# Twelve buffers of fetched edge rows, and sums stored nine steps behind the fetches

## What is computed

```python
h = relu(layernorm(x))
x = x + layer0(h, edge scalars 16, edge vectors 4, gather by src, sum by dst)
h = relu(layernorm(x))
x = x + layer1(h, edge vectors 3, edge features 64, gather by dst, sum by src)

# inside a layer, for every edge e
w   = act(edge_features[e] @ Wfc1) @ Wfc2        # 192 or 224 weights of the edge
f   = node_features[other end of e]              # 160 values of a node
msg = products of w, f and the edge's 3-vector   # 449 or 640 columns
agg[own end of e] += msg                         # segment sum over nodes
```

## Time and profile before

| | |
|---|---|
| time, median of 3 runs | 12249.92 us (12239.58 to 12279.39) |
| the profiled execution, its own time | 12298.2 us |
| its span, first to last instruction | 12296.4 us |
| messages of layer 0, first load to the end of the stage | 2794 to 7956 us |
| messages of layer 1 | 8718 to 12013 us |
| busy: PE, DVE, ACT, POOL | 60%, 61%, 41%, 59% of the span |
| the 16 DMA engines | 107 GB/s on the mean |

### The profile page before, as it was taken

The page is one execution under the profiler, slowest core; times in us unless marked ns, Lnnn a source line. Parts: engine busy times, 40 slices in busy tenths (PEclk is TensorE's granted clock), DMA queues, the critical chain, the costliest instruction groups (busy, mean ns, idle before and its releaser), DMA issues. The chain is left out here.

```text
span 12296.4 us, 187070 instructions
## 1 busy us (share of the span) xinstructions
PE 7410.2 (60%) x31320; PEld 4866.9 (40%) x31320; DVE 7443.2 (61%) x21099; ACT 4992.3 (41%) x16585; POOL 7196.8 (59%) x7101
## 2 busy tenths in 40 slices
PE   4444444445555555555555555577667777777777
PEld 3222222222222222222222222255566666666667
DVE  6444444445565565555555565576667777777763
ACT  2333333333333333333333333343445555555553
POOL 4666666656666666666666666555555666665650
PEclk7555555557777777777777777788899999999999
DMA  2222222223333333333333334444444444444465
GB/s 80 74 74 74 73 73 72 74 69 108 106 109 107 109 110 108 108 109 107 107 108 109 109 108 108 92 148 143 120 116 127 128 122 124 128 128 122 129 114 166
DMA packets 854401, 1321.82 MB, mean 107 GB/s; under 512 B 253376, under 2 KB 655040, under 8 KB 854208
## 3 DMA queue, kind: packets, MB, share of 16 engines
q0 software_dynamic: 339456, 670.10, 20.0%
q1 hardware_dynamic: 469232, 606.08, 17.5%
q10 hardware_dynamic: 45648, 44.94, 1.3%
HBM read 868.56 MB, written 918.54 MB: 145 GB/s over the span
## 5 line engine op out<-in xcount | busy, mean ns | idle before, releaser
L1396 POOL DMA_INDIRECT feat_m<-feat_tab,rows_m x3744 | 3867.9, 1033 | 2929.9 <-DMA rows_m<-sorted_rows 1401.3
L1470 PE MATMUL bank<-prod_m,hot_m 128*128 128x449 f32 x3744 | 2329.6, 761 | 2211.0 <-issue 646.9
L1493 PE MATMUL pair<-prod_m,hot_m 128*128 128x160 f32 x14976 | 2386.6, 316 | 930.1 <-DVE prod_m L1679 621.6
L1493 PEld LDWEIGHTS pair<-prod_m,hot_m 128*128 128x128 f32 x14976 | 2203.1, 201 | 1114.1 <-issue 1114.0
L1526 ACT ACTIVATE prod_m<-part_m,rows_m 128x64 f32<-128x64 f32 x5616 | 1442.4, 337 | 2812.9 <-DVE part_m L1665 1890.2
L1514 ACT ACTIVATE hot_m<-hot_m,rows_m 128x128 f32<-128x128 f32 x5616 | 1742.7, 388 | 1565.9 <-DVE hot_m L1648 1194.7
L600 POOL DMA_INDIRECT sorted_rows<-rows_e,place_e x1664 | 1634.9, 983 | 1051.8 <-issue 520.7
L1470 PEld LDWEIGHTS bank<-prod_m,hot_m 128*128 128x128 f32 x3744 | 858.1, 252 | 3446.1 <-issue 3285.3
L1413 POOL DMA_INDIRECT sorted_rows<-later_m,place_m x1248 | 1274.2, 1021 | 380.9 <-issue 369.9
L1711 DVE SCALAR_TENSOR_TENSOR acc_m<-acc_m,same_block,bank 128x449 f32<-128x449 f32 x936 | 636.5, 680 | 1294.6 <-remote 731.3
L1679 DVE TENSOR_TENSOR prod_m<-rows_m,feat_m 128x192 f32<-128x192 f32 (+1 forms) x4680 | 1226.9, 311 | 0.0
(11 more groups left out here) (241 smaller groups left out, 8767.3 us busy)
## 6 DMA issues: line engine op xcount, KB each, us to landing
agg_tab<-acc_m SPq DMA_DIRECT2D x936, 320.0 KB
rows_m<-sorted_rows SPq DMA_DIRECT2D x936, 229.0 KB
agg_tab<-acc_m SPq DMA_DIRECT2D x936, 224.5 KB
rows_m<-sorted_rows SPq DMA_DIRECT2D x936, 197.0 KB
feat_m<-feat_tab,rows_m POOLq DMA_INDIRECT x3744
turned_m<-in_turned ACTq DMA_DIRECT2D x159, 256.0 KB
agg_s<-agg_tab SPq DMA_DIRECT2D x98, 320.0 KB, 2.7
sorted_rows<-rows_e,place_e POOLq DMA_INDIRECT x1664
```

The lines of the kernel that those rows point to most:

```text
L1396: pool.indirect_dma_start(out=feat[s % RING][:, k, :], out_offset=None, in_=g.feat_tab[l.n], in_offset=bass.IndirectOffsetOnAxis(ap=rows[s ...
L1470: mm = pe.matmul(out[:, 0, :], hot[s % HOTS][:, k, 0, :], prod[s % prods][:, k, 0:l.agg], start=(k == 0), stop=(k == ST_TILES - 1))
L1493: mm = pe.matmul(dst, hot[s % HOTS][:, k, q, :], rhs, start=(k == 0 and col == 0), stop=(k == ST_TILES - 1), skip_group_check=True)
```

## The change

The rows get a ring of twelve buffers, the gathered features keep six under a name of their own (FRING), and the store falls nine steps behind the load. The load of step u now comes right behind the store of step u - 10. The three `acc` buffers stay as they are, and so does every transfer and every instruction of DVE, ACT, PE and POOL. In `sort_edges`, the semaphores on which transfers count are given back last.

```diff
-RING = 6
+RING = 12
+FRING = 6
 HOTS = 3
-STORE_LAG = 5
+STORE_LAG = 9
...
-    for u in used:
+    by_transfers = {u.num for u in (s_zero, s_const, s_in, s_fc, s_w, s_wz, s_neg, *turned_here, *meta_here, *s_key,
+                                    *rows_sent, *stored)}
+    for u in sorted(used, key=lambda v: v.num in by_transfers):
         nc.release_semaphore(u)
...
-        feat = [sb(f"feat{s}", [P, ST_TILES, D], F32) for s in range(RING)]
+        feat = [sb(f"feat{s}", [P, ST_TILES, D], F32) for s in range(FRING)]
...
-        feat_here = [sem(f"feat_here{s}") for s in range(RING)]
+        feat_here = [sem(f"feat_here{s}") for s in range(FRING)]
...
                 pool.wait_ge(rows_here[s % RING], 16 * (use(it, s, RING) + 1))
-                if step is None or step >= RING:
-                    pool.wait_ge(prod_ready, u - RING + 1)
+                if step is None or step >= FRING:
+                    pool.wait_ge(prod_ready, u - FRING + 1)
...
-                        out=feat[s % RING][:, k, :], out_offset=None, in_=g.feat_tab[l.n],
+                        out=feat[s % FRING][:, k, :], out_offset=None, in_=g.feat_tab[l.n],
...
-                f, out_p = feat[s % RING], prod[s % prods]
-                dve.wait_ge(feat_here[s % RING], 16 * ST_TILES * (use(it, s, RING) + 1))
+                f, out_p = feat[s % FRING], prod[s % prods]
+                dve.wait_ge(feat_here[s % FRING], 16 * ST_TILES * (use(it, s, FRING) + 1))
```

More of the change, by code:

```diff
@@ L1396, in gather @@
                     pool.indirect_dma_start(
-                        out=feat[s % RING][:, k, :], out_offset=None, in_=g.feat_tab[l.n],
+                        out=feat[s % FRING][:, k, :], out_offset=None, in_=g.feat_tab[l.n],
                         in_offset=bass.IndirectOffsetOnAxis(ap=rows[s % RING][:, k, l.idx_at:l.idx_at + 1], axis=0)
-                    ).then_inc(feat_here[s % RING], 16)
+                    ).then_inc(feat_here[s % FRING], 16)
             def send(step, it, s):
```

## The result

| | before | after |
|---|---|---|
| median of the runs side by side | 12264.6 us (4 runs) | 12393.85 us (4 runs) |
| ratio | | 1.0094, interval 1.0074 to 1.0114 |
| the profiled execution, its own time | 12298.2 | 12372.25 |
| messages of layer 0, windows | 5162 | 5153 |
| messages of layer 1, windows | 3295 | 3393 |

The kernel is slower by 0.94%. The two profiled executions lie 74 us apart and not 129: that of before took 34 us more than the median beside it, that of the change 22 us less. Each kernel has one traced execution, so stage times of two kernels that lie within some 40 us of each other aren't told apart by the traces alone. The time lies inside the range, but "no difference" was the likeliest case and is wrong, and the slow rival had been put in the wrong layer.

What follows compares the result with a forecast made beforehand. SP's own pace, slowed while POOL issues, was taken to bound both message stages. Ring, lag and gathers counted 0 and the stage ends +20 us: 12250 + 20 = 12270 us, range 12020 to 12450 us.

Steps and rivals of the forecast that it cites:

- no difference: Whole kernel: no change that can be told, 12270 us; the likeliest case, chance 0.46.
- the slow rival: Layer 0: more rows ahead lengthen POOL's bursts, SP crawls longer, stores stop DVE; 174 us more, 12444 us, chance 0.27.
- What bounds the kernel: Both message stages: SP all but never waits, so rows come late because SP itself does, slowed while POOL issues.
- The first rival: DVE's waits for rows and features are the bound and vanish: 11929 us, or 11251 with layer 0 too; chance 0.12.
- The ring: SP's loads, both layers: twelve row buffers remove a wait worth 0 to 11 us; taken as 0.
- The lag's waits: DVE, both layers: waits for features and rows all but vanish, the store takes their place; cost nothing.
- Remote: DVE before additions in layer 0: 731.3 us of waits the profile doesn't name, taken to be mostly the store.
- The gathers: POOL waits more for products, a us or so at a time, at no cost to DVE; taken as 0.
- The ends: Both ends of each stage: four more stores cost 29 us, the start gives back 9; sum +20 us.
- SP shows waits for A(u - 9) in the middle of a stage: Sign in the next profile, SP in the message stages: if seen, SP was not the bound.

Runs made afterwards that it cites:

- the fourth chip: Chip of the last run: the change with twelve feature buffers and without SP's run-time bounds checks; 10013.71 us against 10151.97 for the kernel before, ratio 0.986.
- the repeat: The changed kernel as it stands, run once more beside the kernel before on another chip; 12384.57 us, ratio 1.0089.
- The ring alone: The change with the store lag left at five: twelve buffers of rows, six of features; 12513.14 us, ratio 1.0007.
- twelve features: The change with twelve buffers of gathered features instead of six, repeated on another chip; 12266.86 us, ratio 1.0014.
- six sums: The change with six buffers for the sums instead of three, so an addition waits for the store six steps before; 12310.41 us, ratio 1.0047.
- lag seven: The change with the store seven steps behind the load instead of nine; 12305.06 us, ratio 1.0026.
- the first chip: Where the change with twelve feature buffers was first tried, some semaphores not given back; 12518.9 us, ratio 1.0011 to the kernel before (12507.94 us).
- the change without the bounds checks: The change without the three run-time bounds checks in SP's read of the table; 12125.7 us, ratio 0.9882 to the kernel before.

## Why the prediction was right and wrong

**What bounds the kernel: half right.** SP is a link in a loop with POOL, and that rows come late because SP does stands. On the fourth chip the kernel before takes 17% less, and in the one trace from there SP's instructions are not stretched; that the one makes the other is likely, but the kernel before has no trace on that chip. But "SP never waits, so SP is the bound" was too strong. Adding 0.56 us to its step costs 0.35 and 0.15, and taking 0.75 away gives 0.16 in layer 0 (5009 us against the 5158 of before, first load to last store) and nothing in layer 1. The others stand close behind. The first rival's gain, which came out of the rule that I had set against this reading (the Trainium skill, Perfetto Trace Analysis, section What "DMA-bound" means), did not appear: the trace disagrees with it in so far as SP's register work, which is no DMA slice, decides when rows come.

**The ring: right.** Worth nothing alone (1.0007).

**The lag's waits: right in kind for layer 0.** Features and rows vanished from DVE's waits, in layer 0 the store took their place, and the layer didn't move (5162 to 5153 us, and 5136 in the repeat). DVE fell back as foreseen: in layer 1 the products of a step end 23.8 us after its load is issued (median), where it was 10.0. Two readings were wrong. "Remote" wasn't mostly the store, as shown above. And SP's instructions per step don't stay the same. In layer 1 SP has 15983 instruction records against 15505, nearly all of the difference in the arithmetic for the wait values of a ring twelve long. The ring alone has them too and costs nothing.

**The gathers: this is the step that failed.** I wrote that POOL would wait more for products "by a us or so at a time" and that this "costs DVE nothing, which is behind", and took 0 between a gain of 100 us and the slow rival. It cost 98 and 109 us in layer 1. The 11.3 and 190.2 us from which I started were no waits for P(u - 6) at all: counted by step there were none. The kernels that ran on chips alike, layer 1 from first load to last store, in us:

| kernel | layer 1 | product wait, counted (steps) | product wait by the profile's name | SP stands for a sum, counted | the rest of SP's time |
|---|---|---|---|---|---|
| before | 3293 | 0 | 190 | 61 | 3232 |
| twelve features | 3291 | 0 | 182 | 19 | 3272 |
| six sums | 3304 | 3 (7) | 270 | 5 | 3299 |
| lag seven | 3321 | 0 | 226 | 31 | 3290 |
| the change | 3391 | 275 (180) | 362 | 102 | 3289 |
| the change again | 3402 | 290 (166) | 382 | 133 | 3269 |

The counted wait is there in the two runs that lose 0.9% and all but absent in the others. The change differs from twelve features by 100 and 111 us of layer 1, and SP's standing for sums by 83 and 114 us, while the rest of SP's time is the same within 20 us. So nearly all of what the six feature buffers cost is time in which SP stood for a sum, and not slower work of SP. Against the kernel before the standing is 41 and 72 us longer, and the rest of SP's time 57 and 37.

The road from POOL's wait to the late sum is shown in part. SP runs the store nine steps behind, so DVE's products come four steps later against SP's loads. With six feature buffers POOL waits for them, and so its next transfer starts just when DVE works on: it takes 1.83 and 1.88 us, not 1.10, which comes to 158 and 154 us over an undisturbed 0.95 in each. Then POOL issues in one run what had piled up. Of the 103 and 133 steps in which SP stood for a sum for over 0.15 us, 94 and 122 have a gather that waited for products within two steps, where 54 and 52% of all steps have. It is not that the features are late: they are issued 16 us before their products end (median), and DVE has no waits for them. Why the addition is late after such a run is argued from the stretch above, by SP's wide spacings in it, and not shown.

What I missed is that a lag of nine with six feature buffers leaves POOL no reserve: the gather of step u may be at most six steps ahead of DVE, and DVE had just been put about that far behind. Before, P(u - 6) ended 10.5 us before the load of step u (median); with the change it ends 2.5 us after it. The ring of rows was doubled and the ring of features, behind it, was not. Each link that is loosened alone (features, sums, or two steps of lag) takes the counted wait away and gives most of the layer back.

**The ends: right.** Four more stores behind the last load were to cost 29 us; from last load to last store it is 33.1 and 22.0 us where it was 19.4 and 17.9, so 18 us. The start gave back about what was foreseen, 9 us: the 21st load of a stage comes 5.3 us (layer 0) and 4.2 us (layer 1) sooner after the first than before, and 1.0 and 4.6 us sooner in the repeat. So the ends cost some 8 to 14 us net, against the 20 foreseen. The run in which layer 1's loss is gone is 18 us above before (12266.86 - 12249.26, interval 0 to 0.28%), which fits them and can hardly be told from nothing.

**The slow rival: right in kind, wrong in place.** Its mechanism was longer runs of POOL and an SP that crawls in them, given 0.27 and priced at 174 us, in layer 0. The longer of POOL's runs did get longer, and it cost 98 us, in layer 1, though as standing for sums and not as crawling. In layer 0 no gather waited for products, so nothing was changed there in what starts and ends POOL's runs. I had looked for the rival where SP's spacings were worst, and not where P(u - 6) would come to lie behind the load of step u: one layer 0 step takes 5.5 us and a layer 1 step 3.5, and by the median P(u - 6) still ends 4.0 us before that load in layer 0 and 2.5 us after it in layer 1. Of the marks that I had set, "SP shows waits for A(u - 9) in the middle of a stage" came true and said what it was meant to say.

**Open.** How SP is slowed on three of the chips, and whether POOL's runs do it or only go together with it (below). How POOL's wait and its long transfers make an addition late. A part of DVE's idle time before additions in layer 1 has no cause that the trace shows: it comes after DVE's own last work, PE's last matmul of the step (whose end is modelled) and the store of step u - 3 are all done. Where the addition starts over 0.5 us after the last of these, it amounts to 332 us before, 561 and 538 with the change, 459 with twelve features, and none in the fourth chip's trace. Why twelve features left layer 1 at 3396 us on the first chip, where no gather waited for products either. The 28 us that a lag of seven still costs layer 1. Six sums is 61 us above before in total while its two message stages are 4 and 11 us above; most of this is that the traced execution of before took 47 us more than the median of before on that chip, and that of six sums 9 more than its own. The change as it stands wasn't run on the fourth chip, where, with an SP that doesn't crawl, its lag might cost less or more.

Of what ran, the change without the bounds checks (ratio 0.9882) and the same with twelve feature buffers (0.986, on another chip) beat both kernels.

## What to carry to other kernels

When a ring is deepened, go down the chain of rings behind it and count for each how many steps its consumer may now be late: the shallowest one becomes the next bound, and here it was the one that the diff named beside the other and left at six. An engine without waits is not thereby a bound with a fixed pace; add a known cost to it and see how much comes through before pricing anything by its pace. And where an engine waits for a counter that rises in every step, don't take the profile's name for the wait: look up when the value that was needed had been reached. Here 190 us "for products" were none, and the 275 that were real had to be counted by step.

## What the runs showed of the hardware

SP's register instructions of 0.06 to 0.15 us are now and then stretched to about 0.70 us, or twice that, on three chips, and never in the trace from the fourth (at most 0.16 us). In layer 0 some of DVE's are stretched so too (30 over 0.4 us before, 73 with the change), and none of those of ACT, PE and POOL. Since POOL issued its indirect transfers on the fourth chip back to back over all of layer 0, such issuing alone isn't enough to slow SP; before, I had only seen the two together. The kernel before takes 12250 to 12508 us on the three and 10152 on the fourth, and DVE, ACT and POOL are busy as long in the traces of both kinds of chip.

An indirect transfer of layer 1 takes POOL 0.95 us when DVE does nothing beside it, or only an addition. Where it overlaps the one-hot and both groups of products it takes 1.36 us on the mean (408 of 1397 between 9000 and 11500 us in the changed kernel; before, 216 of 1436, at 1.30), and up to 2.5. The Trainium skill (SBUF — State Buffer, section SBUF: two separate sides) says that GpSimd can't write the descriptors of a DMA that it issues while a DVE operation holds the port pair that the two share; the durations agree with that in kind. The page tells it of DVE operations in a two-port mode, and no run here shows whether these are. Which of them coincide depends on who lets POOL go. In these 2500 us the coinciding ones took 168 us more than as many undisturbed ones would have, before 76; these 92 us are most of the additional busy time (154 us in the whole layer).

PE's granted clock falls to 1.2 GHz in many short stretches. In layer 1 they add up to 332 us before, 656 with the change and 556 with twelve features, the last at no loss of time.
